# Two gated attentions: one pipelined loop over pairs of head groups, tiled score and value products, VectorE copies

## The reference

```
x = rms_norm(hidden, ln_in_w)
mixed = where(vm, x @ v_qkv, x @ l_qkv)          # two experts, chosen per token
q, k, v = split(mixed); q, k = apply_rotary(q, k)  # 16 heads of 16
ctx = sdpa(q, k, v, causal=True)
hidden = hidden + where(vm, ctx @ v_dense, ctx @ l_dense)
ci = rms_norm(hidden, ln_post_cross_w)
cq = heads(ci @ cq_w); ck, cv = heads(encoder @ ckv_w)  # 16 heads of 8
hidden = hidden + sdpa(cq, ck, cv, causal=False) @ cdense_w
```

## Time and profile before

| | us |
|---|---|
| median of three runs | 1572.76 (1571.05 to 1575.96) |
| the profiled execution | 1576.42 |
| its span, first to last instruction | 1574.5 |
| PE busy | 1472.0 (93%) |
| PE weight loads busy | 1242.7 (79%) |
| DVE busy | 914.9 (58%) |
| ACT busy | 706.8 (45%) |
| POOL busy | 370.1 (24%) |
| mean granted TensorE clock | 0.975 |

### The profile page before, as it was taken

One profiled execution on the slowest core, in us unless ns is written; L12 is line 12 of the kernel. 1 busy time (PEld: TensorE's weight loads), 2 busy tenths in 40 slices (PEclk: granted clock), 3 DMA queues, 4 the chain that ended last, 5 costly groups with the idle time before them and its releaser, 6 DMA issues.

```text
span 1574.5 us, 31313 instructions
## 1 busy us (share of the span) xinstructions
PE 1472.0 (93%) x10850; PEld 1242.7 (79%) x10850; DVE 914.9 (58%) x2003; ACT 706.8 (45%) x2277; POOL 370.1 (24%) x472
## 2 busy tenths in 40 slices
PE   5889899899989989999998999998998999999899
PEld 4757676767767768999987888887987788887899
DVE  3546664655655677566545555656663555556664
ACT  2324344334433446222246665566335565566432
POOL 0135323324414420000003222331011222223100
PEclk9999999999999988999999999999998999999999
DMA  4203000000000002000010000001000100000000
GB/s 154 67 20 114 4 1 3 3 0 0 7 0 1 1 1 88 1 0 0 1 54 5 5 7 3 3 1 60 28 0 1 59 7 3 3 3 1 5 23 27
DMA packets 13226, 30.21 MB, mean 19 GB/s; under 512 B 2400, under 2 KB 8800, under 8 KB 12512
## 3 DMA queue, kind: packets, MB, share of 16 engines
q1 hardware_dynamic: 13152, 29.23, 5.3%
HBM read 27.13 MB, written 2.10 MB: 19 GB/s over the span
## 4 chain that ended last, share of the span: by engine, by line
PE 62%; issue 20%; POOL 8%; DVE 7%; ACT 2%; DMA 0%; SPq 0%; POOLq 0%; DVEq 0%; ACTq 0%
PE bank L828 55%; PE bank L841 7%; POOL p L1736 2%; POOL xT L1736 1%; POOL kbd L1736 1%; POOL rstd L1694 1%; DVE pT L1209 1%; DVE stats L1239 1%; DVE nmax L1310 1%; DVE xn L1285 1%; POOL kbd L1727 1%; DVE xn L1289 0%; DVE xn L1287 0%; DVE x_all L1342 0%; DMA p<-in_media 0%
## 5 line engine op out<-in xcount | busy, mean ns | idle before, releaser
L1548 ACT ACTIVATE p<-bank,nmax 128x128 f32<-128x128 f32 x512 | 146.8, 370 | 261.2 <-DVE nmax L1310 260.8
L1310 DVE TENSOR_REDUCE nmax<-bank 128x4 f32<-128x512 f32 x256 | 170.3, 686 | 130.0 <-PE bank L828 129.6
L828 PE MATMUL bank<-w_ff_rounded,hT_rounded 128*128 128x256 f32 x944 | 218.1, 286 | 7.4 <-ACT w_ff_rounded L1658 2.6
L1209 DVE COPY pT<-bank 128x512 f32<-128x512 f32 x256 | 169.7, 683 | 90.3 <-PE bank L841 89.8
L828 PE MATMUL bank<-kbd,hT 64*128 64x128 f32 (+1 forms) x1280 | 203.6, 340 | 5.0 <-ACT hT L1493 3.9
L828 PE MATMUL bank<-xT_rounded,w_ff_rounded 128*128 128x256 f32 x864 | 197.2, 286 | 3.7 <-issue 2.4
L828 PE MATMUL bank<-xT_rounded,kbd_rounded 128*128 128x256 f32 x608 | 173.5, 285 | 0.0
L828 PE MATMUL bank<-xn_rounded,w_ff_rounded 128*128 128x256 f32 x608 | 172.9, 284 | 0.0
L828 PEld LDWEIGHTS bank<-w_ff_rounded,hT_rounded 128*128 128x128 f32 x944 | 163.5, 193 | 9.1 <-ACT v L1493 3.0
L841 PEld LDWEIGHTS bank<-consts,p 128*128 128x128 f32 x784 | 94.5, 143 | 77.1 <-issue 69.4
L828 PEld LDWEIGHTS bank<-xT_rounded,w_ff_rounded 128*128 128x128 f32 x864 | 149.8, 193 | 5.1 <-issue 5.1
(11 more groups left out here) (160 smaller groups left out, 3071.9 us busy)
## 6 DMA issues: line engine op xcount, KB each, us to landing
ctxT<-in_ctxT SPq DMA_DIRECT2D x32, 128.0 KB, 2.4
w_ff<-in_w1b SPq DMA_DIRECT2D x6, 640.0 KB, 6.6
w_att<-in_w2a SPq DMA_DIRECT2D x1, 3072.0 KB, 10.9
w_att<-in_w3a SPq DMA_DIRECT2D x1, 3072.0 KB, 10.2
w_att<-in_w1a SPq DMA_DIRECT2D x1, 2432.0 KB, 11.1
hT<-in_xT SPq DMA_DIRECT2D x8, 256.0 KB, 3.0
o<-in_x SPq DMA_DIRECT2D x8, 256.0 KB, 3.1
w_ff<-in_w2b SPq DMA_DIRECT2D x1, 2048.0 KB, 7.8
```

The costliest lines, as they stand in the source:

```text
L828: return pe.matmul(dst, lhsT, rhs, start=first, stop=last)
L1209: dve.tensor_copy(dst, src).then_inc(sems[s[0], "copied"], 1)
L1310: dve.tensor_reduce(nmax[:, ph.place[s] % P_RING, :], bank[:, :].rearrange("p (h t) -> p h t", h=QUAD), AX_X, ALU.max, negate=True).then_i ...
L1548: t = act.activation(p[:, part], bank[:, part], ACT.Exp, bias=nmax[:, i, j:j + 1])
```

## The change

The two attentions become one list of 16 slots per iteration (`gated_slots`), in the order cross A, self A (of the next iteration), cross B, self B (of the next iteration), with one pair of groups (c = 0, 1) of one row in each slot. In slot k stand: the mix of pair k - 4, the turns of pair k - 3, the scores of pair k, and the share of pair k - 1. The other steps are given to fixed slots by `gated_sides`: 8 lists of three places (in front, before the scores, after them) for each half of the iteration. Steps of self attention are all early, so the two self attentions of the first iteration run as a prologue behind phase 0, and the two cross attentions of the last iteration stay for the end, where the rounding of the expert weights for phase 2 is spread between them.

- Scores: the keys are spread only within the 64 rows (self) or 32 rows (cross) that hold a group's features, and the two groups of a pair use different rows of the array. GpSimd's spreads have 512 columns in place of 1024: six for each unit in place of eight.
- Sums: ACT's exponential accumulates them, DVE inverts them for a pair (`share`), and GpSimd multiplies the probabilities in place (two instructions of 512 columns for a pair).
- Values (`mix`): each head's values are padded to 32 columns and stationary; `pT` moves, 128 columns. Four strips of 32 columns of the array take four heads, two heads after one another add up in each strip. The result is the context already transposed, and normalised, so `maskedT` and `coT`'s transposes, `mask` and the normalising are gone. All mixes use bank 7; DVE copies a row's context out (`ctx`, 128x256, and `coT`, 128x128; before, ACT copied those).
- `dense` takes both experts in one bank of 512 columns for a row, and DVE adds them with two masked instructions.
- Scores keep four banks for themselves, and the other jobs three (4 to 6).
- GpSimd clears all of `v` at the start, and the cross dense weights come in 16 small DMAs, in the order of the strips.

`norm_q` and `norm_ff` become one name, `norm_ln`, without other work.

```diff
+def gated_slots():
+    quads = [("cross", A_, 0), ("self", A_, 1), ("cross", B_, 0), ("self", B_, 1)]
+    pairs = [((kind, u, b, c), early) for kind, u, early in quads for b in range(ROWS) for c in range(GROUPS // 2)]
+    n = len(pairs)
+    def of(k, steps):
+        pair, early = pairs[k % n]
+        return [(s, early + k // n) for s in steps(*pair)]
+    def mix(kind, u, b, c):
+        done = [({"self": "ctx", "cross": "coT"}[kind], u, b)] if c == GROUPS // 2 - 1 else []
+        return [(of_kind("mix", kind), kind, u, b, c)] + done
     slots = []
-    for i in range(len(groups) + SKEW_O):
-        slot = []
-        if i < len(groups):
-            slot += here(("scores",) + groups[i])
-        if 0 <= i - SKEW_T < len(groups):
-            slot += here(("turn",) + groups[i - SKEW_T])
-        if 0 <= i - SKEW_O < len(groups):
-            slot += here(("values",) + groups[i - SKEW_O])
-        slots.append(slot)
+    for k in range(n):
+        slots.append((of(k - 4, mix) + of(k - 3, lambda *pair: groups_of("turn", pair)),
+                      of(k, lambda *pair: groups_of("scores", pair))
+                      + of(k - 1, lambda *pair: groups_of("share", pair)[0:1])))
...
+def gated_sides():
+    def part(u):
+        v, of_v = (B_, here) if u == A_ else (A_, ahead)
+        keys_a, keys_b = (ahead(*spreads("self", u)[b * DC:(b + 1) * DC]) for b in range(ROWS))
+        keys_c = of_v(*spreads("cross", v))
+        return [(ahead(("norm_self", u)), [], ahead(("scale_self", u))),
+                ([], ahead(("xvT", u), ("xlT", u)), []),
+                ([], [], ahead(("qk", u, 0), ("qk", u, 1), ("qkT", u, 0)) + keys_a[:1]),
+                ([], of_v(("dense", v, 0)) + keys_a[1:], of_v(("dense", v, 1), ("norm_cross", v))),
+                ([], ahead(("v1", u)) + of_v(("scale_cross", v)) + ahead(("qkT", u, 1)) + keys_b, []),
+                ([], of_v(("nT", v), ("ck", v)), keys_c[:1]),
+                ([], [], here(("cdense", u, 0), ("half", u))),
+                ([], of_v(("cv", v), ("cq", v)) + keys_c[1:], here(("cdense", u, 1), ("end", u)))]
+    return part(A_) + part(B_)
...
+        if index == 1:
+            of_scores = [s for s in jobs if s[0].startswith("scores")]
+            mixes = [s for s in jobs if s[0] in ("mix", "mix_cross")]
+            others = [s for s in jobs if s not in of_scores + mixes]
+            self.bank = {s: i % QUAD for i, s in enumerate(of_scores)} | {s: BANKS - 1 for s in mixes}
+            self.bank |= {s: QUAD + i % (BANKS - QUAD - 1) for i, s in enumerate(others)}
...
+            def scores_gated(ph, it, s):
+                name, kind, u, b, g = s
                 w = views[u]
+                banks = [ps[ph.bank[s[:4] + (g + i,)]] for i in range(2)]
                 if kind == "self":
+                    c = g // 2
+                    pe.wait_ge(*after(ph, it, ("qkT", u, b), "copied"))
+                    pe.wait_ge(*after(ph, it, ("spread_self", u, b, c), "done"))
+                    settle(pe, "tensor")
+                    for bank in banks:
+                        mm(bank[:, :], ident16[:, :], causal16[:, :].unsqueeze(1).broadcast_to([P, QUAD, P]), True, False)
+                    for i, bank in enumerate(banks):
+                        part = slice(i * HD2, (i + 1) * HD2)
+                        mm(bank[:, :], w.qT1[part, b, c, :], w.k1[part, b, c, :, :], False, True).then_inc(sems[name, "mm"], 1)
+                else:
                     pe.wait_ge(*after(ph, it, ("cq", u), "copied"))
+                    pe.wait_ge(*after(ph, it, ("spread_cross", u, b), "done"))
+                    settle(pe, "tensor")
+                    for i, bank in enumerate(banks):
+                        part = slice((g + i) * STRIP, (g + i + 1) * STRIP)
+                        mm(bank[:, :], w.cqT[part, b * P:(b + 1) * P], w.ck1[part, b, :, :], True, True)\
+                            .then_inc(sems[name, "mm"], 1)
...
-                    t = mm(bank[:, j * w:(j + 1) * w], pT_ring[ph.place[s] % PT_RING][:, j * P:(j + 1) * P],
-                           v_view(kind, u)[:, b, g * QUAD + j, :], True, True)
+            def mix(ph, it, s, bank):
+                kind, u, b, c = s[1:]
+                pe.wait_ge(*after(ph, it, (of_kind("turn", kind), kind, u, b, 2 * c + 1), "copied"))
+                pe.wait_ge(*after(ph, it, ("v1" if kind == "self" else "cv", u), "copied"))
+                for i in range(2):
+                    for j in range(QUAD):
+                        strip = slice(j * STRIP, (j + 1) * STRIP)
+                        if kind == "self":
+                            head = 2 * j + i
+                            t = mm(bank[strip, c * P:(c + 1) * P], v_strip(kind, u, b, c * HDC + head),
+                                   pT_ring[head // QUAD][:, head % QUAD * P:(head % QUAD + 1) * P], i == 0, i == 1)
+                        else:
+                            group = 2 * c + i
+                            t = mm(bank[strip, 0:P], v_strip(kind, u, b, group * QUAD + j), pT_ring[i][:, j * P:(j + 1) * P],
+                                   group == 0, group == GROUPS - 1)
...
-                turn(s, ph.bank[s], [xn[u][:, b, e, c * P:(c + 1) * P] for e in range(EXPERTS) for c in range(DC)])
+                at, chunks, width = W1A["dense0"]
+                both = w_att[:, at:at + EXPERTS * chunks * width].rearrange("p (e c n) -> p c e n", e=EXPERTS, c=chunks)
+                pe.wait_ge(*after(ph, it, ("ctx", u, b), "copied"))
+                for c in range(DC):
+                    t = mm(bank[:, :], views[u].ctxT[:, b, c, :], both[:, c, :, :], c == 0, c == DC - 1)
...
+            def ctx(ph, it, s, bank):
+                u, b = s[1:]
+                job = ("mix", "self", u, b, DC - 1)
+                dve.wait_ge(*after(ph, it, job, "mm"))
+                dve.tensor_copy(views[u].ctxT[:, b, :, :], ps[ph.bank[job]][:, 0:D].rearrange("p (c t) -> p c t", c=DC)).then_inc(sems[s[0], "copied"], 1)
+            def coT(ph, it, s, bank):
+                u, b = s[1:]
+                job = ("mix_cross", "cross", u, b, GROUPS // 2 - 1)
+                dve.wait_ge(*after(ph, it, job, "mm"))
+                dve.tensor_copy(views[u].coT[:, b, :], ps[ph.bank[job]][:, 0:P]).then_inc(sems[s[0], "copied"], 1)
...
+                for e, event in enumerate(("half", "added")):
+                    if e:
+                        dve.wait_ge(*after(ph, it, s, "half"))
+                    dve.scalar_tensor_tensor(out=x_b, in0=bank[:, e * D:(e + 1) * D].unsqueeze(1),
+                                             scalar=vm_here[:, u, b, e:e + 1], in1=x_b,
+                                             op0=ALU.mult, op1=ALU.add).then_inc(sems[s[0], event], 1)
...
-                dve.reciprocal(rinv[:, i % 2, :], r[:, :, w - 1]).then_inc(sems[s[0], "rinv"], 1)
-                dve.wait_ge(*after(ph, it, s, "rinv"))
-                dve.tensor_tensor(out_of(kind, u, b, g), r[:, :, 0:w - 1],
-                                       rinv[:, i % 2, :].unsqueeze(2).broadcast_to([P, QUAD, w - 1]), ALU.mult).then_inc(sems[s[0], "normed"], 1)
...
-                    else:
-                        t = act.activation(p[:, part], bank[:, part], ACT.Exp, bias=nmax[:, i, j:j + 1])
+                    t = act.activation(p[:, part], bank[:, part], ACT.Exp, bias=nmax[:, g, j:j + 1],
+                                       accum_out=rsum[:, g, j:j + 1])
...
+            def spread_self(ph, it, s, bank):
+                u, b, c = s[1:]
+                w = views[u]
+                pool.wait_ge(*after(ph, it, ("qkT", u, b), "flat"))
+                pool.wait_ge(*after(ph, it, ("scores", "self", u, b, 2 * c + 1), "exp", back=1))
+                src = w.k_flat[:, (DC * b + c) * P:(DC * b + c + 1) * P]
+                pool.tensor_tensor(w.k1[:, b, c, :, :], src.unsqueeze(1).broadcast_to([P, QUAD, P]),
+                                        rows_self[:, :].unsqueeze(2).broadcast_to([P, QUAD, P]), ALU.mult).then_inc(sems[s[0], "done"], 1)
...
-                        for kind in ("self", "cross"):
-                            t = pool.memset(v_view(kind, u)[:, :, :, head_width(kind)], 1.0)
+                        t = pool.memset(v[u][:, :], 0.0)
...
-            sp.dma_start(w_att[:, 0:W1A_COLS], dram["w1a"]).then_inc(weights_att, 16)
+            at = W1A["cdense"][0]
+            sp.dma_start(w_att[:, 0:at], dram["w1a"][:, 0:at]).then_inc(weights_att, 16)
+            for j in range(QUAD):
+                for n in range(GROUPS):
+                    to, row_at = j * STRIP + n * HDC, (n * QUAD + j) * HDC
+                    sp.dma_start(w_att[to:to + HDC, at:at + D], dram["w1a"][row_at:row_at + HDC, at:at + D])\
+                      .then_inc(weights_att, 16)
```

More of the change, by code:

```diff
@@ L136, in media_slots, with gated_body @@
+def gated_body():
+    return [front + first + early + second + late
+            for (first, second), (front, early, late) in zip(gated_slots(), gated_sides())]
```

(14 more changed lines are left out.)

321 lines of the change are left out of this document (139 added, 182 removed), and 4 rows, old and new, of the table EVENTS.

## The result

The changed kernel takes 1513.2 us (median of 4 runs, 1507.7 to 1517.1), the kernel before 1574.4 beside it; the ratio is 0.961, 95% interval 0.956 to 0.965. In a second series of five runs it took 1508.7, ratio 0.957 (0.955 to 0.959). Forecast were 1498, and 1450 to 1540 as the range. The profiled execution took 1517.1, with a span of 1515.3.

The account below looks back on a forecast made before the run. PE was taken as the bound, busy for 93% of the span. Three steady iterations (58 us) and the ends (17) took the profiled 1576.4 to 1501.4; the median, 3.6 below, gave 1498 us, range 1450 to 1540.

Parts of the forecast that it names:

- The cost of the tiles: PE's attention products: 1.11 us a mix (bounds 0.53 to 1.81), 1.46 a pair's scores (1.04 to 1.90); a self pair 3.87.
- one pack: Rival: tiles in PE's array overlap as one pack, scores 1.04 and mix 0.53 us a pair, total 1434 us; chance 0.12.
- The losses: PE's waits and time at 1.2 GHz in an iteration: 8 us lost in place of 12.7.
- The stall: PE waits for scaled `xn` at the `xvT` transposes, 1.2 to 3.5 us, twice an iteration.
- clock falls: Rival: in slots of narrow tiles and transposes PE's granted clock goes to 1.2 GHz, total 1658 us; chance 0.06.
- chain binds the thin slots: Rival: each of four thin slots a half lasts a pair's 6.3 us chain, iteration 117 us, total 1543; chance 0.16.
- The ends: Self attentions alone at the start, cross alone at the end: 124.4 us with losses of 28, 17 us less than before.
- Copies, `v` clear, DMAs at nothing: Context copies on VectorE, clearing `v` and 16 DMAs cost nothing; late copies some 3 us an iteration, clears at most few us.
- the three iterations: Steady state of the attention loop: 104.4 us an iteration, 19.4 less than before, 58 us for three.

## Why the prediction was right, and where it wasn't

**The cost of the tiles was mis-sized.** The sum had 1.11 for a mix and 1.46 for a pair's scores; they cost 0.58 and 1.06, near the lower bounds (0.53, 1.04). Of the rival "one pack" both prices hold, not its 1434. A self pair is 0.58 + 0.93 + 0.52 + 1.06 = 3.09 us, not 3.87. The work is 87.3 us an iteration, not 96.4; the prices of mix and scores alone would have made it 81.5. The other 5.8 lie in what I had left at its old price. By the starts of the rows in the iteration from 279.17, the masks cost 0.8 more than forecast and the turns nearly 2; the other 3 or so are the remaining work, where short pieces between the tiles cost more than long ones: a 256-column instruction 0.31 us in a group of two and 0.216 in one of sixteen.

**The losses were halved and should not have been.** The sum took 8 us an iteration: 5 of waits and 3 of the lower level. They are 7.1 and 7.8. The stall itself came where it was foreseen, twice an iteration, with 2.3 to 2.6 us (forecast 1.2 to 3.5), for the reason given (scalings of 2.71 us beside a share). Its price in clock was mis-sized. The one wait of the earlier trace rows already cost about 3 us of clock: 6.69 for 16 instructions that take 3.62 at the upper level in the kernel after. I counted these 3 once for two waits. Here a wait costs 3.9.

**So 102.1 for 104.4 is two errors that cancel**, 9 us too much work and 7 us too few losses. That the number fits so well is luck; the stall and its cause were foreseen. The rival "clock falls" was wrong in its mechanism, as the narrow tiles run at 2.4 GHz for over 20 us on end, but half right on the price: a short wait among them is dear. Two slips in what I wrote on it change nothing here: 44 us an iteration at half speed would be 176 us in four, not 160; and the 4.1 us of media tiles and turns (902.30 to 906.42) hold a dense product of two instructions, at 904.25. The rival "chain binds the thin slots" holds in a small part, 0.5 to 0.8 us for `pT` ahead of one mix a half.

**The ends saved nothing, and 17 us were forecast.** I left their losses at 28 us; they are 140.7 - 87.3 = 53. By the rows shown first, 29.3 are idle (12.4 and 16.9), 18.6 are half of the time at the lower level (clocks of 0.85 and 0.88), and 5.5 are other work in these stretches, the gate's product among it. About 4 to 5 are the gate's product behind the waiting transposes; the rounding is worth 1. The rest I take to be the chain of a pair with little beside it: self alone at the start, cross alone at the end, each now with half the PE work to hide it. The waits of 3.99 us for the exponentials fit, but no run tests that part.

**Copies, `v` clear, DMAs at nothing**: right for the copies within a few microseconds; the others were not tried apart.

**Where the phases behind stand.** From the first expert product to the end it was 963.4 us before and 969.8 after, with the same code. PE's work in the same place is the same, the clock isn't: in steps of half a microsecond, it is at the lower level for 31.3 us of this stretch after and for 18.4 before, and 13 us at half speed are the 6.5 that it is longer. For one place of it, the 60 us that start 420 us behind that product, after:

```profile
965.46:1025.46 60.00, 53.19 (x494) 45.73 (x490) 36.19 (x71) 37.90 (x133) 16.83 (x19) 0.97 0.00 1
```

and in the kernel before:

```profile
1031.15:1091.15 60.00, 52.93 (x508) 45.32 (x507) 37.68 (x75) 39.65 (x136) 16.82 (x19) 1.00 0.00 1
```

So 65.7 us won by 545 us became 59 in that execution. Against the forecast of 75: the three iterations gave 65 (58 forecast), the ends nothing (17), and the phases behind, forecast at nothing, took 6.5 back. Over all traces here this stretch varies from 961 to 970 us. Why the level falls at a seam in one kernel and not in another stays open.

## What to carry to other kernels

Where narrow tiles fill PE's stream, a wait of a little over two microseconds can cost more than itself: behind each wait of 2.3 to 2.6 us in the changed kernel's loop the clock was down for 3.4 to 10.2 us, and about half of that was lost. So once the tiles are cheap, look first for the engine that ends such a wait, and keep long GpSimd instructions from running beside the VectorE work it needs; here that order was worth 31 to 36 us, about half as much as the change itself. And a saving of PE work shows only where other work hides the chain: count it for the full iterations, not for the ends.

## What the hardware showed unexpectedly

- Products on separate strips overlap nearly fully, in fp32 too and in either order: 16 instructions of 128 columns take 1.87, 1.02 and 0.58 us on one, two and four strips.
- With scores on all rows the clock fell less. There, behind six waits of 2.13 to 2.57 us, PE stayed at the upper level four times and was at the lower one for 3.4 us twice; with row tiles, behind the six waits of 2.34 to 2.62 us in each of the changed kernel's two traces, it was at the lower one for 3.4 to 10.2 us every time. The length of the wait alone doesn't decide it: with the copies on ACT a wait of 2.62 us had no such result and one of 2.34 had, and with unit B's norm moved the same wait of 2.23 us was once followed by the upper level and once not. The condition stays open.
- VectorE's scalings took either 0.27 us or, beside a GpSimd multiplication of about 1.1 us, as long as that one.
- Adding 21 us of PE work an iteration lengthened it by 8 (102.1 to 110.5), as the waits grew shorter and the clock stayed up.
